# A ResNet block's last pass: low parts of the two recomputed pairs made by GpSimd instead of VectorE

## The reference

```python
def block(x, w1, b1, gamma1, beta1, w2, b2, gamma2, beta2):
    identity = x
    out = conv3x3(x, quantize_weight(w1, 8), b1)
    out = relu(batchnorm(out, gamma1, beta1))       # mean and var over all 32 images
    out = conv3x3(out, quantize_weight(w2, 8), b2)
    out = batchnorm(out, gamma2, beta2)
    return relu(out + identity)

x = x + block(group_norm(x, G=32), ...)             # x: (32, 64, 56, 56) float32
```

## Time and profile before

| | before |
|---|---|
| median of 3 runs | 526.12 us (525.89 to 526.38) |
| the profiled execution | 526.89 us |
| its span | 525.1 us |
| granted TensorE clock, mean | 0.987 |
| TensorE busy | 494.5 us (94%) |
| VectorE busy | 451.3 us (86%), 648 instructions |
| ScalarE busy | 368.8 us (70%), 410 instructions |
| GpSimd busy | 85.9 us (16%), 155 instructions |
| last pass | from about 404 us to the end |

### The profile page before, as it was taken

How to read it: one execution, slowest core, us unless ns; L and a number is a source line. 1 busy time by engine, 2 the same in 40 slices (tenths; PEclk the granted TensorE clock), 3 DMA queues, 4 the chain that set the end, 5 groups by cost and what they waited for, 6 DMA issues and landing times.

```text
span 525.1 us, 23736 instructions
## 1 busy us (share of the span) xinstructions
PE 494.5 (94%) x11003; PEld 424.4 (81%) x11003; DVE 451.3 (86%) x648; ACT 368.8 (70%) x410; POOL 85.9 (16%) x155
## 2 busy tenths in 40 slices
PE   4999999999999999999999999999997888979994
PEld 2899999999999787899888888898886466567552
DVE  7999989999999966998888898878796989988874
ACT  3899799999999964766655565566622799677472
POOL 2027256666651200000000000000001000000000
PEclk9999999999999999999999999999998999979998
DMA  8934775533333000001343300000056899999997
GB/s 276 362 131 130 257 265 175 196 134 134 131 135 129 10 9 7 2 4 64 136 172 142 128 2 4 4 2 4 2 180 257 324 402 413 428 385 422 382 415 328
DMA packets 23098, 92.99 MB, mean 177 GB/s; under 512 B 8152, under 2 KB 9560, under 8 KB 18776
## 3 DMA queue, kind: packets, MB, share of 16 engines
q1 hardware_dynamic: 22816, 91.19, 45.8%
q10 hardware_dynamic: 184, 0.30, 0.2%
HBM read 58.27 MB, written 32.28 MB: 172 GB/s over the span
## 4 chain that ended last, share of the span: by engine, by line
PE 88%; DVE 5%; issue 2%; ACT 2%; DMA 1%; SPq 1%; DVEq 0%; ACTq 0%
PE conv_ps L1409 71%; PE conv_ps L1531 6%; PE conv_ps L1554 5%; PE conv_ps L1577 4%; DVE slots L1288 1%; DMA slots<-in_x_dram 1%; DVE slots L1294 1%; PE conv_ps L1539 1%; DVE bn_tup L1097 1%; SPq L371 1%; DVE split L1317 0%; ACT split L623 0%; ACT split L818 0%; DVE xa L1310 0%; DMA slots<-slots 0%
## 5 line engine op out<-in xcount | busy, mean ns | idle before, releaser
L1409 PE MATMUL conv_ps<-split,wmat 64*64 64x385 f16 (+3 forms) x9216 | 380.4, 324 | 2.2 <-ACT split L623 1.8
L1409 PEld LDWEIGHTS conv_ps<-split,wmat 64*64 64x64 bf16 x9216 | 345.2, 107 | 33.6 <-issue 3.3
L657 ACT ACTIVATE slots<-conv_ps,par,evac_scale 128x784 f32<-128x784 f32 x124 | 123.7, 998 | 94.0 <-PE conv_ps L1409 92.3
L1097 DVE BATCH_NORM_STATS2 bn_tup<-slots 128x6 f32<-128x392 f32 x164 | 80.8, 554 | 12.8 <-ACT slots L657 12.8
L984 DVE BATCH_NORM_STATS2 small<-slots 128x6 f32<-128x448 f32 x112 | 61.8, 612 | 1.3 <-DMA slots<-in_x_dram 1.3
L1062 DVE TENSOR_TENSOR split<-slots,split 128x3136 f16<-128x3136 f32 (+4 forms) x36 | 57.2, 1606 | 3.9 <-ACT slots L637 0.9
L1064 DVE SCALAR_TENSOR_TENSOR split<-slots,split 128x3248 f16<-128x3248 f32 (+3 forms) x18 | 53.6, 2978 | 2.3
L1040 DVE TENSOR_SCALAR slots<-slots,bn_w 128x3248 f32<-128x3248 f32 (+3 forms) x18 | 30.4, 1687 | 19.7 <-ACT split L613 19.1
L613 ACT ACTIVATE split<-slots,bn_w 128x3248 f16<-128x3248 f32 x14 | 43.2, 3082 | 0.0
L665 ACT ACTIVATE xa<-conv_ps,par,evac_scale 128x784 bf16<-128x784 f32 x40 | 39.7, 994 | 0.0
L1554 PE MATMUL conv_ps<-split,wmat 64*64 64x385 f16 (+3 forms) x576 | 29.5, 346 | 7.1 <-ACT split L818 3.4
(11 more groups left out here) (159 smaller groups left out, 417.4 us busy)
## 6 DMA issues: line engine op xcount, KB each, us to landing
slots<-in_x_dram SPq DMA_DIRECT2D x13, 1568.0 KB, 12.1
slots<-in_x_dram SPq DMA_DIRECT2D x51, 392.0 KB, 5.2
out_dram<-slots SPq DMA_DIRECT2D x7, 1568.0 KB, 7.3
out_dram<-slots SPq DMA_DIRECT2D x10, 784.0 KB, 8.5
y_spill<-slots SPq DMA_DIRECT2D x3, 1624.0 KB, 6.2
slots<-y_spill SPq DMA_DIRECT2D x3, 1624.0 KB, 6.8
xa<-in_x_dram SPq DMA_DIRECT2D x2, 1568.0 KB, 11.5
split<-in_x_dram SPq DMA_DIRECT2D x2, 1568.0 KB, 10.0
```

The source lines that it names most:

```text
L657: nc.scalar.activation(dst, src, ACT.Identity, bias=bias, scale=scale, accum_out=total).then_inc(evacuated[ph], 1)
L1097: ins = nc.vector.bn_stats(bn_tup[:, 2 * (n - first) + s, :], rows[s])
L1409: return nc.tensor.matmul(bank[:, r0:r1, w0:w1], lhs, rows[:, top + r0:top + r1, w0 + kx - 1:w1 + kx - 1], start=n == 0 and part is hi_all ...
```

## The change

`again_low1` moves from VectorE's list to GpSimd's. GpSimd runs the four halves one after the other behind its last instruction, each with the same waits (`again_act1`, `again_hi1`) and the same semaphore for TensorE and ScalarE (`again_lo1`). In half 1 it makes the 224 columns first, waits for them (`again_rest`), and then makes the 1008 columns. VectorE's list is otherwise as it was.

```diff
+        again_rest = sem("again_rest")
...
@@ gpsimd, behind part_diag @@
+            def again_low1(r, n):
+                pool.wait_ge(again_act1, 2 * r + n + 1)
+                pool.wait_ge(again_hi1, 2 * r + n + 1)
+                views = [again_parts(again1[r][:, 1], n), again_parts(again_fp32[r], n), again_parts(again1[r][:, 0], n)]
+                if n == 1:
+                    nc.gpsimd.tensor_tensor(*(v[1] for v in views), ALU.subtract).then_inc(again_rest, 1)
+                    pool.wait_ge(again_rest, r + 1)
+                nc.gpsimd.tensor_tensor(*(v[0] for v in views), ALU.subtract).then_inc(again_lo1, 1)
+                pool.wait_ge(again_lo1, 2 * r + n + 1)
+
+            pool.wait_ge(part_diag_ready, 2)
+            for r in range(len(AGAIN)):
+                for n in range(2):
+                    again_low1(r, n)
...
@@ vector @@
-            def again_low1(r, n):
-                dve.wait_ge(again_act1, 2 * r + n + 1)
-                dve.wait_ge(again_hi1, 2 * r + n + 1)
-                for l, a, h in zip(again_parts(again1[r][:, 1], n), again_parts(again_fp32[r], n), again_parts(again1[r][:, 0], n)):
-                    ins = nc.vector.tensor_tensor(l, a, h, ALU.subtract)
-                ins.then_inc(again_lo1, 1)
...
             for r, (first, second, third) in enumerate(((4, 5, 6), (8, 9, 10))):
                 u = AGAIN[r]
-                again_low1(r, 0)
-                again_low1(r, 1)
                 two_pass(first, 0)
                 two_pass(first, 1)
```

## The result

The changed kernel takes 528.49 us (median of 5 runs, 527.52 to 530.23), the kernel before 525.89 us beside it (5 runs). The ratio is 1.0062, 95% interval [1.0037, 1.0087]: slower by 0.6%, some 3 us. The direction was forecast, and 528.49 lies in the range of 527.5 to 534.8; the likeliest case said 530.5, and its own range of 529 to 532 begins above the measured time.

What follows compares the result with a forecast made beforehand. TensorE's chain of work in the last pass was taken to bound the kernel, not VectorE. Pair 7's 1.8 us and pair 11's 2.6 us gave +4.4 us on the median of 526.12, so 530.5 us; range 527.5 to 534.8.

Steps and rivals of the forecast that it cites:

- the likeliest case: First rival, chance 0.40: GpSimd's subtraction in pair 11 held up by one VectorE operation; 530.5 us.
- TensorE's order is the end's order; VectorE's 7.3 us are worth nothing.: Last pass: TensorE's losses between 426 and 497 reach the end; the 7.3 us taken off VectorE gain nothing.
- GpSimd's length, 4.2 us.: Large low part, 1904 columns: the subtraction takes GpSimd 4.2 us, at 2.1 ns a column.
- The bounds of 1.8 and 7.3 us: Low and high end for GpSimd's large subtraction, from its memsets and its smallest subtractions.
- Pair 7, +1.8 us.: Pair 7: TensorE starts the low part at 430.5 instead of 428.75, +1.8 us.
- Pair 11, +2.6 us, held by one VectorE operation.: Pair 11: GpSimd is held until VectorE's L1288 ends, so the low part starts 2.6 us late.
- Two small terms of unlike sign I let cancel.: Round 0's low part longer at half clock (+0.5 to +1), against instruction-side gaps of about 1 us a pair partly used up.
- the second rival: Pair 11, chance 0.20: GpSimd gets in beside VectorE, not held up; +2.7 us, 528.8 us.
- fourth rival: Pair 7, chance 0.07: TensorE's stop of 2.3 us lowers the clock; +2.7 us, 533.2 us.
- ScalarE's delays by the small parts.: Both pairs: ScalarE's act2 waits for GpSimd's small parts, slipping up to 1.5 us against TensorE in pair 11, covered by 4 us.

Runs made afterwards that it cites:

- e4_small: Kernel before with only the small low parts (224 and 1008 columns) of both pairs made by GpSimd; 1.0005 of the kernel before.
- e2_pair7: Kernel before with only pair 7's low parts made by GpSimd, pair 11's left on VectorE; 1.0026 of the kernel before, +1.4 us.
- e5_nohold: Changed kernel, but in pair 11 VectorE waits for both halves of the low part before its first step of place 8; 1.0018 of the kernel before.
- e12_pair11_nohold: Kernel before with only pair 11's low parts on GpSimd, VectorE waiting for them before its first step of place 8; 0.9994 of the kernel before.
- e7_late11: Kernel before with pair 11's large subtraction done twice by VectorE, GpSimd doing none; 0.9991 of the kernel before.
- e6_late7: Kernel before with pair 7's large subtraction done twice by VectorE, GpSimd doing none; 1.0022 of the kernel before, +1.2 us.
- e9_thin_after: Changed kernel with most transfers from place 4 of the last pass on cut to 196 columns; 0.9912 of the kernel before.
- e1_after: The changed kernel timed again with no edit, 12 runs; 528.25 against 525.48 us for the kernel before, ratio 1.0054.
- e10_thin_late7: Kernel before with most transfers from place 4 on cut to 196 columns and pair 7's large subtraction done twice by VectorE; 0.9856 of the kernel before.

## Why the prediction was right in direction, and too high

- **TensorE's order is the end's order; VectorE's 7.3 us are worth nothing.** Held. e4_small took 3 us of work off VectorE for no change. In the changed kernel VectorE is only 2.4 us less busy (451.3 to 448.9 us), as 1.9 + 3.5 us of the gain went into the two rows that GpSimd held up, and its earlier start in pair 11 did harm.
- **GpSimd's length, 4.2 us.** Measured 3.81 us when alone, 2.0 ns a column where 2.1 was taken; the estimate from two to three memset streams was good, though the 2.1 was a choice between 1.7 and 2.5. The 4.18 us estimated from the Trainium skill (GPSIMD Engine Reference, Performance versus the Vector engine) was 10% too high as well. The bounds of 1.8 and 7.3 us were much wider than needed, but nothing in the trace of before could narrow them.
- **Pair 7, +1.8 us.** The stop grew by 1.48 us; the 0.3 us less is GpSimd's shorter length. At the end 1.4 us (e2_pair7).
- **Pair 11, +2.6 us, held by one VectorE operation.** The mechanism came as described, up to L1304 starting 0.33 us before GpSimd and GpSimd going first when L1304 was done. It was 2.04 us late: 0.4 us less by GpSimd's shorter length, and 0.2 us less as L1304 had a lead of 0.33 us, not 0.1. e5_nohold and e12_pair11_nohold show that the hold is all of pair 11's cost that can be measured.
- **"Two small terms of unlike sign I let cancel."** The lateness, corrected for the above, sums to 3.5 us, and 2.8 us came out, with an interval of 1.6 to 4.1: the difference isn't clear of noise, so the cancelling held, but by luck. Both terms were there, and neither was small. The gaps give back 1.0 + 1.4 = 2.4 us by the table above, where a part of about 1 us in each pair was taken; the profile of before had the rows, seven gaps of 5.0 us, and I counted most of them as fixed, as if they were work. The clock takes about as much away again: 0.984 instead of 0.988 over 526 us is some 4.2 us more at the lower level, and at 1.33 us lost in the 3.30 us of a high part that is 1.7 us, an estimate, and a high one, as TensorE stands still in a part of that time. 3.5 - 2.4 + 1.7 = 2.8. The two aren't independent: the runs of e7_late11 have a mean clock of 0.985 against 0.989 and lost no time, with only 0.8 us of gaps behind pair 11's low part, so what the lower clock costs there the gaps gave back. How the loss divides between them stays open.
- **So what made the forecast 1.6 us too high** is, as far as the runs tell, the sizes in the sum: 0.9 us from GpSimd's length and the hold (4.4 against 3.5), and 0.7 us that may be noise or the balance of gaps and clock.
- **A right time for another reason.** 528.5 is nearly what the second rival gives (528.8, GpSimd not held up). The rows refute that case: 5.16 us against 3.81, and L1310 at 5.27.
- **The clock behind pair 7's stop (fourth rival).** It didn't fall in the profiles of the changed kernel. It did in e2_pair7, e6_late7 and e9_thin_after, with stops of 2.0, 2.7 and 2.0 us:

```profile
428.00:430.00 2.00, 0.21 (x8) 1.00 1.02 422
430.00:432.00 2.00, 2.00 (x74) 0.78 1.08 445
432.00:434.00 2.00, 2.00 (x35) 0.50 0.98 420
434.00:436.00 2.00, 2.00 (x48) 0.87 1.02 433
```

  These are e2_pair7's stretches (from:to, length, TensorE busy (x), granted clock, DMA share, GB/s). In the changed kernel's profile the clock stays at 1.00 through the same stop. So the fall is a matter of the single execution. Its price can be read: from pair 7's first low matmul to the first of the second convolution it is 442.09 - 429.79 = 12.30 us in e2_pair7 and 440.96 - 430.24 = 10.72 us in e1_after, where the clock stays up, with no gap in either, so 1.6 us, where 2.7 was forecast. It may be why the changed kernel's runs scatter more (527.5 to 530.2). How many of the timed runs had it isn't known.
- **ScalarE's delays by the small parts.** `make_act2(1, 0)` ran at 471.10 instead of 468.30, 4.95 us of waiting for GpSimd, and nothing came of it, as forecast.

No version here with all its transfers is faster than the kernel before; the best, e12_pair11_nohold, e7_late11 and e4_small, are even with it.

## What to carry to other kernels

An engine's busy share says nothing on what it is worth to unload it: ask whether what it makes arrives last where it is used, and if so, never give that piece to a slower engine. If VectorE work does move to GpSimd, look at what VectorE does in the time it gains: an operation with two SBUF operands started just before GpSimd's holds up the very result that others wait for, and one wait on VectorE took that cost away. And gaps without a cause that grow with the data transfers aren't fixed work; a new stop ahead of them is paid for in part by them. A new stop can also keep the clock low for longer, so a sum of stops alone comes near the truth only when the two happen to balance.

## What the runs showed of the hardware

- GpSimd's `tensor_tensor` (f32 minus f16 to f16, 128 partitions): 3.81 us for 1904 columns, 2.10 for 1008, 0.61 for 224, so 1.9 ns a column and 0.18 us; VectorE 2.14 us for the 1904.
- GpSimd and VectorE excluded one another for whole instructions, in both directions, in the cases here, where both read two operands from SBUF: VectorE's 1.74 and 1.79 us became 3.62 and 5.27 us, GpSimd's 3.81 and 0.61 us became 5.16 and 2.04 us. The trace of before had shown only one direction, on operations of one column. The Trainium skill (SBUF — State Buffer, Who interferes with whom) says that a VectorE instruction with two SBUF inputs contends with a GpSimd one that reads SBUF, and that the order of issue decides which of them waits; the trace agrees with both.
- TensorE loses 1.9 to 5.1 us in gaps without a shown cause between 426 and 497 while the DMA engines are fully busy (ten profiles), and nothing when they are nearly idle (four).
- A stop of 2.0 us on TensorE was followed by the lower clock in e2_pair7 and e9_thin_after and not in after, e1_after and e5_nohold; one of 2.7 us was in e6_late7 and not in e10_thin_late7.
